# Routing rows by comparisons, identity products in the gate logits, a group score by maxima and minima, and running sums over tiles by TensorE

## The reference, cut to what matters

```python
logits = x @ gate_w.T                      # x: 2048 rows of 256, after the layer norm; 64 experts
scores = jax.nn.sigmoid(logits)
scores_for_choice = scores + gate_bias[None, :]
grp = scores_for_choice.reshape(T, NG, E // NG)            # 8 groups of 8 experts
group_scores = jnp.sum(jax.lax.top_k(grp, 2)[0], axis=-1)  # sum of the two largest of a group
_, gidx = jax.lax.top_k(group_scores, TOPK_GROUP)          # the best 4 groups
gmask = jnp.zeros((T, NG), dtype=scores.dtype).at[jnp.arange(T)[:, None], gidx].set(1.0)
emask = jnp.repeat(gmask, E // NG, axis=1)
masked = jnp.where(emask > 0, scores_for_choice, 0.0)
_, topk_idx = jax.lax.top_k(masked, TOP_K)                 # 8 experts of a row
topk_w = jnp.take_along_axis(scores, topk_idx, axis=1)
topk_w = topk_w / (jnp.sum(topk_w, axis=-1, keepdims=True) + 1e-20) * ROUTED_SCALE
out = routed + shared     # routed: the 8 chosen experts, weighted; shared: two experts for every row
```

## Time and profile before

| | us |
|---|---|
| median of 3 runs | 1512.27 (1512.11 to 1514.17) |
| the profiled execution's own time | 1514.72 |
| its span, first to last instruction | 1512.9 |
| TensorE busy in the span | 1364.1 |
| VectorE busy | 861.2 |
| ScalarE busy | 692.9 |
| GpSimd busy | 514.6 |

### The profile page before, as it was taken

One profiled execution on the slowest core, in us unless ns is written; L12 is line 12 of the kernel. 1 busy time (PEld: TensorE's weight loads), 2 busy tenths in 40 slices (PEclk: granted clock), 3 DMA queues, 4 the chain that ended last, 5 costly groups with the idle time before them and its releaser, 6 DMA issues. The chain is left out here.

```text
span 1512.9 us, 30501 instructions
## 1 busy us (share of the span) xinstructions
PE 1364.1 (90%) x8093; PEld 1070.4 (71%) x8093; DVE 861.2 (57%) x2301; ACT 692.9 (46%) x1847; POOL 514.6 (34%) x570
## 2 busy tenths in 40 slices
PE   4988969999999999999566799999998899999998
PEld 3876636777777777777344567776765799999997
DVE  6878964333333333333337567667678576666666
ACT  2444303444444444444024577677776444444443
POOL 1001323333333333331554477656662111111110
PEclk8877969999999999999787899999999899999999
DMA  4016115768566557643422122221120000000000
GB/s 104 0 54 170 26 33 161 219 191 241 160 202 185 174 161 218 192 115 93 128 86 64 57 57 65 59 66 50 44 87 22 10 13 15 15 14 14 14 7 15
DMA packets 107710, 136.12 MB, mean 90 GB/s; under 512 B 29843, under 2 KB 91635, under 8 KB 107603
## 3 DMA queue, kind: packets, MB, share of 16 engines
q1 hardware_dynamic: 64643, 61.15, 13.9%
q0 software_dynamic: 15456, 48.62, 12.0%
q10 hardware_dynamic: 27504, 25.05, 4.9%
HBM read 102.75 MB, written 32.01 MB: 89 GB/s over the span
## 5 line engine op out<-in xcount | busy, mean ns | idle before, releaser
L769 POOL DMA_INDIRECT xg<-n_rows,idx x191 | 181.1, 948 | 314.9 <-DVE wS L2110 218.5
L1269 PE MATMUL ps<-wgu,xT 128*128 x764 | 260.6, 464 | 0.6 <-ACT xT L1070 0.6
L1269 PE MATMUL ps<-wdn,hT 88*128 x764 | 198.4, 382 | 2.5 <-DVE hT L2119 2.5
L2287 DVE TENSOR_REDUCE nmx<-ps 128x1 f32<-128x333 f32 x256 | 127.1, 498 | 123.3 <-PE ps L1269 118.8
L1147 ACT ACTIVATE pD<-ps,nmx 128x333 f32<-128x333 f32 x256 | 139.2, 546 | 98.6 <-DVE nmx L2287 75.6
L2116 DVE TENSOR_TENSOR hC<-sg,ps 128x176 f32<-128x176 f32 x203 | 68.5, 337 | 185.1 <-ACT sg L1080 162.2
L2119 DVE COPY hT<-ps 88x256 f32<-88x256 f32 x203 | 85.4, 421 | 152.4 <-issue 86.9
L1269 PEld LDWEIGHTS ps<-wgu,xT 128*128 128x128 f32 x764 | 130.8, 191 | 42.5 <-issue 2.0
L1587 PE MATMUL ps<-ident,pD 128*128 128x128 f32 x768 | 130.9, 281 | 28.2 <-DVE pT L2293 16.0
L786 POOL DMA_INDIRECT yg<-y_rows,slotG x128 | 123.4, 964 | 93.3 <-ACT pD L1147 33.7
L1080 ACT ACTIVATE sg<-ps 128x176 f32<-128x176 f32 x191 | 60.6, 318 | 185.4 <-PE ps L1269 179.2
(11 more groups left out here) (310 smaller groups left out, 3084.7 us busy)
## 6 DMA issues: line engine op xcount, KB each, us to landing
y_rows<-yC ACTq DMA_DIRECT2D x191, 128.0 KB
wgu<-in_wgu SPq DMA_DIRECT2D x64, 352.0 KB
wdn<-in_wdn SPq DMA_DIRECT2D x64, 176.0 KB
xg<-n_rows,idx POOLq DMA_INDIRECT x191
...
```

Source lines behind the costliest of these rows:

```text
L769: pool.indirect_dma_start(out=xg[:, b % XS, :], out_offset=None, in_=n1_rows, in_offset=bass.IndirectOffsetOnAxis(ap=idx[:, b:b + 1], axis ...
L1269: return pe.matmul(o, lhsT, rhs, start=start, stop=stop, **kw)
L2287: dve.tensor_reduce(nmx[:, k:k + 1], ps[:, score_bank(k), 0:NK1], AX, ALU.max, negate=True).then_inc(d_mx, 1)
```

## The change

Five things change.

1. The group score: the count and the second maximum are replaced by a small network of pairwise maxima and minima over halves of a group.
2. cselb is gone. TensorE adds up the tiles instead: each tile's selb, repeated, is multiplied by ones into all the tiles that follow it. Places for the first half are made behind step 1 (places_early), the rest behind step 3.
3. ohP is made for a whole tile by one comparison, as ohB is, without the row number; parH takes the place of parF. ScalarE multiplies the tile's ohP by the row number in place (numbered()), two tiles at the end of each of its steps 6 to 9 and the rest after step 9. TensorE waits for that (b_ohn), and tells VectorE of used buffers once a tile and no longer once a product.
4. TensorE makes products of the identity with itself, whose results nobody reads: one of 256 columns for every two gate tiles, five in each of the last two tiles of the first attention, ten behind it.
5. VectorE's second clearing of qP (two memsets) is gone, the late steps stand in another order among the sums of gathered rows, and SyncE waits for the gathered rows of the second tile before it loads the context's values.

```diff
...
@@ -645,2 +643,3 @@
             sp.wait_ge(d_zero, ZERO_PIECES)
+            sp.wait_ge(k_ld[1], 16 * TOPK)
             load_values(0)
...
@@ -1056,5 +1055,22 @@
             s_copy_xT(0, 0)
-            pairs(act, s_step, n=NSE)
+
+            def numbered(n):
+                rows = ohP[:, n % OHS, :, :].rearrange("p k n -> p (k n)")
+                act.wait_ge(b_oh, 2 * n + 1)
+                act.activation(rows, rows, ACT.Copy, scale=id1[:, n:n + 1]).then_inc(b_ohn, 1)
+
+            for t in range(2):
+                s_step(t, t, 0)
+            with act.Fori(1, FILL_AT // 2) as i:
+                for r in range(2):
+                    s_step(2 * i + r, r, i)
+            for t in range(FILL_AT, NSE):
+                s_step(t, t % 2, t // 2)
+                for s in range(2):
+                    numbered(2 * (t - FILL_AT) + s)
             s_copy_hT(NSE - 1)
+            numbered(2 * (NSE - FILL_AT))
             s_y_out(NSE - 1, 1, NSE // 2 - 1)
+            for n in range(2 * (NSE - FILL_AT) + 1, NT):
+                numbered(n)
 
...
@@ -1277,2 +1293,8 @@
             pe.wait_ge(const_ready, 2)
+            two_idents = ident[:].unsqueeze(1).broadcast_to([P, 2, P])
+
+            def keep_busy(bank, n):
+
+                for _ in range(n):
+                    mm(ps[:, bank, 0:2 * P], ident[:], two_idents, True, True)
 
...
@@ -1299,2 +1321,4 @@
                     a_scores(t + 2, r, i + 1)
+                else:
+                    keep_busy(1 + 2 * r, 5)
                 if not (isinstance(t, int) and t + 3 >= NT):
...
@@ -1317,2 +1341,3 @@
             pairs(pe, a_step, ahead=4)
+            keep_busy(4, 10)
 
...
@@ -1339,2 +1364,4 @@
                 last.then_inc(b_l, 1)
+                if t % 2:
+                    keep_busy(4, 1)
 
...
@@ -1396,9 +1423,31 @@
 
-            def places():
+            HT = NT // 2
+
+            def counts(half):
+
+                for t in range(half * HT, (half + 1) * HT):
+                    last = mm(ps[:, 7, 0:E0], onesb[:], selb[:, t, :], t == 0, t == NT - 1, skip_group_check=True)
+                return last
+
+            def of_tiles_ahead(half):
+
+                for t in range(HT - 1):
+                    rest = HT - 1 - t
+                    last = mm(ps[:, POS[half], (t + 1) * E0:HT * E0], onesb[:],
+                              selb[:, half * HT + t, :].unsqueeze(1).broadcast_to([P, rest, E0]), False, t == HT - 2, skip_group_check=True)
+                return last
+
+            def places_early():
                 pe.wait_ge(b_sel, 1)
-                HT = NT // 2
-                for g in range(2):
-                    mm(ps[:, POS[g], :], triu[:], selb[:, g * HT:(g + 1) * HT, :], True, False)
-                    mm(ps[:, POS[g], :], onesb[:], cselb[:, g * HT:(g + 1) * HT, :], False, True)
-                mm(ps[:, 7, 0:E0], onesb[:], cselb[:, NT, :], True, True).then_inc(b_pos, 1)
+                mm(ps[:, POS[0], :], triu[:], selb[:, 0:HT, :], True, False, skip_group_check=True)
+                of_tiles_ahead(0)
+                for t in range(HT):
+                    mm(ps[:, POS[1], :], onesb[:], selb[:, t, :].unsqueeze(1).broadcast_to([P, HT, E0]), t == 0, False, skip_group_check=True)
+                counts(0)
+
+            def places():
+                pe.wait_ge(b_sel, 2)
+                counts(1)
+                mm(ps[:, POS[1], :], triu[:], selb[:, HT:NT, :], False, False, skip_group_check=True)
+                of_tiles_ahead(1).then_inc(b_pos, 1)
 
...
@@ -1413,7 +1462,9 @@
             def onehots(t, r):
+                pe.wait_ge(b_oh, 2 * t + 2)
+                pe.wait_ge(b_ohn, t + 1)
                 for k in range(TOPK):
-                    pe.wait_ge(b_oh, TOPK * t + k + 1)
                     start = isinstance(t, int) and t == 0 and k == 0
                     stop = isinstance(t, int) and t == NT - 1 and k == TOPK - 1
-                    mm(ps[:, POS[1], 0:NBLK], ohP[:, r, k, :], ohB[:, r, k, :], start, stop).then_inc(b_ohu, 1)
+                    last = mm(ps[:, POS[1], 0:NBLK], ohP[:, r, k, :], ohB[:, r, k, :], start, stop)
+                last.then_inc(b_ohu, 1)
 
...
@@ -1422,2 +1473,3 @@
             s_step(1, 1, 0)
+            places_early()
             with pe.Fori(1, PLACES_AT // 2) as i:
...
@@ -1995,9 +2047,15 @@
 
-                own.link(dve.tensor_reduce(m1_, sfc_, AX, ALU.max))
-                own.link(dve.tensor_tensor(t1_, sfc_, of_group(m1_), ALU.is_equal))
-                own.step(dve.tensor_reduce(cnt_, t1_, AX, ALU.add))
-                own.link(dve.scalar_tensor_tensor(out=t2_, in0=t1_, scalar=NEG, in1=sfc_, op0=ALU.mult, op1=ALU.add))
-                own.step(dve.tensor_reduce(m2_, t2_, AX, ALU.max))
-                own.link(dve.tensor_scalar(two_, cnt_, 2.0, None, ALU.is_ge))
-                own.link(dve.copy_predicated(m2_, two_, m1_))
+                def of_two(out, a, b, op):
+                    return dve.tensor_tensor(out, a, b, op)
+
+                own.step(of_two(t1_[:, :, 0:4], sfc_[:, :, 0:4], sfc_[:, :, 4:8], ALU.max))
+                own.link(of_two(t1_[:, :, 4:8], sfc_[:, :, 0:4], sfc_[:, :, 4:8], ALU.min))
+                own.step(of_two(t2_[:, :, 4:6], t1_[:, :, 4:6], t1_[:, :, 6:8], ALU.max))
+                own.step(of_two(t2_[:, :, 2:4], t1_[:, :, 0:2], t1_[:, :, 2:4], ALU.min))
+                own.link(of_two(t2_[:, :, 0:2], t1_[:, :, 0:2], t1_[:, :, 2:4], ALU.max))
+                own.step(of_two(t2_[:, :, 2:4], t2_[:, :, 2:4], t2_[:, :, 4:6], ALU.max))
+                own.step(of_two(m2_, t2_[:, :, 0], t2_[:, :, 1], ALU.min))
+                own.link(of_two(m1_, t2_[:, :, 0], t2_[:, :, 1], ALU.max))
+                own.link(of_two(cnt_, t2_[:, :, 2], t2_[:, :, 3], ALU.max))
+                own.link(of_two(m2_, m2_, cnt_, ALU.max))
                 own.link(dve.tensor_tensor(gs_.rearrange("p t g -> p (t g)"), m1_, m2_, ALU.add))
...
@@ -2014,7 +2072,4 @@
                 own.wait()
-                own.link(dve.tensor_tensor(selb_, rep_, masked, ALU.not_equal))
-                for t in range(tiles.start, tiles.stop):
-                    own.link(dve.tensor_tensor(cselb[:, t + 1, :], cselb[:, t, :], selb[:, t, :], ALU.add))
-                if tiles.stop == NT:
-                    dve.memset(cumB[:], 0.0).then_inc(b_sel, 1)
+                dve.tensor_tensor(selb_, rep_, masked, ALU.not_equal).then_inc(b_sel, 1)
+                dve.wait_ge(b_sel, 1 + tiles.start * 2 // NT)
 
...
@@ -2027,3 +2082,4 @@
 
-            own.link(dve.memset(cselb[:, 0, :], 0.0))
+            own.step(dve.memset(cumB[:], 0.0))
+            own.link(dve.memset(cumA[:], 0.0))
             for half_of in (slice(0, NT // 2), slice(NT // 2, NT)):
...
@@ -2034,4 +2090,3 @@
             PAD = E0 // 2
-            own.link(dve.memset(cumA[:], 0.0))
-            dve.wait_ge(b_sel, 1)
+            dve.wait_ge(b_sel, 2)
             dve.wait_ge(b_pos, 1)
...
@@ -2075,15 +2130,16 @@
             own.link(dve.tensor_scalar(slotI[:], slotI[:], P - 1, None, ALU.bitwise_and))
-            own.step(dve.tensor_copy(parF[:], slotI[:]))
+            own.step(dve.tensor_copy(parH[:], slotI[:].unsqueeze(2).broadcast_to([P, NT * TOPK, 2])))
             own.link(dve.tensor_copy(blkH[:], blkI[:].unsqueeze(2).broadcast_to([P, NT * TOPK, 2])))
-            TWOS = [P, TOPK, NBLK // 2, 2]
             end()
 
+            def rows_of_a_tile(out, iota, number, t, n):
+                twos = [P, TOPK, n // 2, 2]
+                return dve.tensor_tensor(out.rearrange("p k (n a) -> p k n a", a=2),
+                                         iota[:].rearrange("p (n a) -> p n a", a=2).unsqueeze(1).broadcast_to(twos),
+                                         number[:, bass.ds(TOPK * t, TOPK), :].unsqueeze(2).broadcast_to(twos), ALU.is_equal)
+
             def onehots(t, r):
-                after(dve, b_ohu, TOPK * (t - OHS + 1))
-                dve.tensor_tensor(ohB[:, r, :, :].rearrange("p k (n a) -> p k n a", a=2),
-                                  iotaB[:].rearrange("p (n a) -> p n a", a=2).unsqueeze(1).broadcast_to(TWOS),
-                                  blkH[:, bass.ds(TOPK * t, TOPK), :].unsqueeze(2).broadcast_to(TWOS), ALU.is_equal)
-                for k in range(TOPK):
-                    u = TOPK * t + k
-                    dve.tensor_scalar(ohP[:, r, k, :], iotaP[:], col(parF, u), col(id1, t), ALU.is_equal, ALU.mult).then_inc(b_oh, 1)
+                after(dve, b_ohu, t - OHS + 1)
+                rows_of_a_tile(ohP[:, r, :, :], iotaP, parH, t, P).then_inc(b_oh, 1)
+                rows_of_a_tile(ohB[:, r, :, :], iotaB, blkH, t, NBLK).then_inc(b_oh, 1)
 
...
@@ -2094,3 +2150,3 @@
                     onehots(OHS * i + r, r)
-            dve.wait_ge(b_ohu, TOPK * NT)
+            dve.wait_ge(b_ohu, NT)
             begin()
...
@@ -2393,7 +2449,5 @@
             dve.tensor_scalar(bproj[:], bproj[:], tg[:, 1:2], None, ALU.mult).then_inc(d_gate, 1)
```

(6 more changed lines are left out.)

12 lines of the change are left out of this document (5 added, 7 removed).

## The result

The changed kernel takes 1519.25 us in the median of 8 runs (1515.61 to 1521.58); the kernel before takes 1513.01 beside it (8 runs, 1512.11 to 1515.30). The ratio is 1.003, with a 95% interval of 1.0018 to 1.0041: **0.3% slower** (the two medians by themselves lie 6.2 us apart), where 0.4% faster was forecast and 1514 was the upper end of the range.

A forecast was written before the change was run, and what follows sets the result against it. VectorE was taken to bound the routing stage, TensorE's fixed list close under it, and TensorE the experts. Gains of 1.1 us (routing) and 5.6 us (between experts and second attention), together 6.7, took 1512.27 to 1505.6 us; range 1494 to 1514.

The forecast's parts named there:

- VectorE's early savings: Routing stage, group score: selb about 1 + 2 us sooner in the first half, counted at nothing because VectorE then waits for TensorE.
- nbI waits for TensorE: Routing stage: VectorE's nbI, at 153.23 without waiting before, now waits for TensorE's place counts until 155.6.
- the scaling: Routing stage: ScalarE multiplies a tile's 1024 one-hot elements by the row number, 1.11 us (bounds 0.69 and 1.2).
- the turns: Routing steps 6 to 9: TensorE and ScalarE wait for each other, 1.73 us behind each step, a round 8.3 us.
- the place products: Routing stage, TensorE: running sums behind step 1 take 3.5 us, behind step 3 1.5 instead of 0.90; counts 3.9 us late.
- the landing of the row tile: Before TensorE's step 2: row tile from DRAM lands at 137.54, queued behind expert weights; no routing work moves it.
- the sum: Routing stage's forecast times added up to its end: 212.1 instead of 213.16, gain 1.1 us.
- the clock at 1.00 from 142 to 200: Routing stage: sign expected in the profile after, TensorE's granted clock staying at full speed through steps and one-hot products.
- rival (d): Routing steps: TensorE's clock falls in the turns, steps 7 to 9 some 13 us more, tail 2; 1521; chance 0.10.
- the second place: Between experts and second attention: memsets gone (2.1 us), late steps ahead of the sum of gathered rows (3.45); gain 5.6 us.
- rival (c): Between experts and second attention: no gain, sums behind the steps cost what the order brings; 1511.2; chance 0.13.
- a rival for a further gain: Between experts and second attention: long waits on remote vanish, 12 us more gained, 1493.6; chance 0.15.

## Why the prediction was wrong

Forecast -6.7 us, measured about +4.5 by the ratio (0.3% of 1513) and +6.2 by the two medians.

1. **The path was right.** VectorE's early savings are worth nothing, nbI waits for TensorE, the scaling costs 1.14 us, the turns are 1.69 us, the place products 3.57. From the landing of the row tile to nbI the sum gave 18.1 us (five profiles: 18.9), to the first one-hot row 31.9 (32.8).
2. **The step that failed first: "the clock at 1.00 from 142 to 200".** I had rival (d), the clock falling in the turns, at 0.10, because "the repeated full-width products of the steps speak for it". It fell in the first turn. From landing to isz the sum had 74.6 us; the five profiles have 83.6, and 77.2 with three products in each turn. So about 6.5 of the 9 us missing are the clock, some 2.5 are small excesses, mostly at nbI and the first one-hot row. The earlier trace rows held the warning: the level had fallen where TensorE waited for every tile. They also leave out 166 to 200, and there the kernel before had lost the clock in its own first round of one-hot products. TensorE's timeline, and the stretch with all engines:

```profile
167.53 0.26 PE L1269 MATMUL ps<-ohB,ohP 128*128 128x192 f16 x1 [0.77 <-DVE ohP L2088]
168.26 1.68 PE L1269 MATMUL ps<-ohB,ohP 128*128 128x192 f16 x7 [0.47 <-DVE ohP L2088]
170.70 1.90 PE L1269 MATMUL ps<-ohB,ohP 128*128 128x192 f16 x8 [0.75 <-DVE ohP L2088]
```

```profile
169.00:175.00 6.00, 5.25 (x17) 2.67 (x18) 6.00 (x22) 0.00 (x0) 0.00 (x0) 0.50 0.00 0
```

   Two waits of less than 0.8 us came before that fall and one behind it. Rival (d)'s time, 1521, lies near the measured 1519.25, but by luck: it put 15 us on the clock, which cost 6 to 7, and kept the 5.6 us of the second place, which were not there.
3. **A term at nothing: the landing of the row tile.** I had written that "no routing work moves it", and of the last attention tile: "up to 1.7 us sooner or 2 later, and the row stores hang on it; I take 0". The landing follows the end of the attention: 36.8 us behind vA with the changed routing part, 39.8 without (means of five). Of these 3 us, 1.7 are the row stores, which start that much sooner with the identity products (the upper bound that I had named); the rest is not told apart from the spread of the loads. That gave 3 us back, at a place where I had put zero. With points 1 and 2, -1.1 + 9 - 3 = +4.9, against the measured +4.3 from vA to isz.
4. **The second step that failed: 5.6 us at the second place.** Worth zero on each chip with remote waits, which is rival (c), at 0.13. I counted steps of 2.4 us and treated the waits on remote as a rival for a further gain; they set when the late steps end (about 36 us from the first sg to the eighth in 13 profiles of 15, with or without the memsets and the sum in between), and what stood between the steps was hidden under them. The earlier trace rows showed both, a wait of 13.70 us beside the 3.45 that I took for path. On the chip without them the steps run as I said.
5. For these waits the prediction cited a rule (the Trainium skill, Runtime: NRT & Kernel Launch, Instruction fetch mechanics: blocks of instructions come over a DMA queue of the engine's own) and drew from it that they would fall on other instructions in a changed program. Mostly they did not. In all 15 profiles that have them the longest on ScalarE, 13.1 to 15.9 us, stands before the same instruction, the eighth sg of the late steps; others come and go before the seventh sg, the hT of the sixth to eighth step and xT, and the total between experts and attention is 20 to 35 us. The profile of the changed kernel counts two instruction queues among its DMA queues, and neither brings a packet between 714 and 760, where the waits of 7.02 and 15.82 us end. That speaks against the rule as their cause, as far as these two queues go. No run here shows what they wait for.
